# Two of a mixer chunk's 16 products delta·u·B are taken from VectorE: a transfer spreads delta·u over the states and GpSimd multiplies it by B

## The reference, cut to what matters

```python
delta = softplus(dt_r @ dt_proj_w + dt_proj_b)
dA  = exp(delta[..., None] * A)                # decay, per channel and state
dBu = delta[..., None] * Bm[:, :, None, :] * u[..., None]
h_t = dA_t * h_{t-1} + dBu_t                   # scan over the 1024 tokens
y_t = sum_n h_t[:, n] * C_t[n]   (+ u * D_param)
```

## Time and profile before

| | us |
|---|---|
| median of 3 runs (lowest, highest) | 3076.52 (3069.46, 3086.7) |
| the profiled execution, its own time | 3082.83 |
| its span in the profile | 3081.0 |
| the mixer's scans, first start to last end | 670.6 to 2519.1 |
| FFN 1 ahead of them, FFN 2 behind | 670 and 562 |
| DVE, POOL, PE busy over the span | 2644.2, 2136.8, 2641.8 |

### The profile page before, as it was taken

One profiled execution on the slowest core, in us unless ns is written; L12 is line 12 of the kernel. 1 busy time (PEld: TensorE's weight loads), 2 busy tenths in 40 slices (PEclk: granted clock), 3 DMA queues, 4 the chain that ended last, 5 costly groups with the idle time before them and its releaser, 6 DMA issues. The chain is left out here.

```text
span 3081.0 us, 31455 instructions
## 1 busy us (share of the span) xinstructions
PE 2641.8 (86%) x10275; PEld 1371.3 (45%) x10275; DVE 2644.2 (86%) x2499; ACT 1693.9 (55%) x2273; POOL 2136.8 (69%) x1284
## 2 busy tenths in 40 slices
PE   4999999967878878878878878878877669999998
PEld 2666656633324424424424424424412216666665
DVE  7888865549999999999999999999999986777775
ACT  3554444446666666666666666666664534444443
POOL 4666654258788788788788788788788755555653
PEclk9999999979969979979979979979976779999999
DMA  3011111057877777777777777776777750110100
GB/s 110 31 52 52 41 48 41 21 136 173 189 182 174 190 183 168 187 191 169 183 191 170 188 185 172 186 188 172 181 180 171 183 143 24 35 35 28 34 28 21
DMA packets 173218, 387.95 MB, mean 126 GB/s; under 512 B 22544, under 2 KB 90064, under 8 KB 172816
## 3 DMA queue, kind: packets, MB, share of 16 engines
q1 hardware_dynamic: 154176, 365.49, 47.9%
q10 hardware_dynamic: 18896, 20.65, 2.3%
HBM read 308.33 MB, written 52.56 MB: 117 GB/s over the span
## 5 line engine op out<-in xcount | busy, mean ns | idle before, releaser
L1428 POOL TENSOR_TENSOR mix_scan<-mix_scan,mix_bc 128x1024 f32<-128x1024 f32 x512 | 1205.3, 2357 | 379.0 <-DVE mix_scan L1512 378.4
L1512 DVE TENSOR_TENSOR_SCAN mix_scan<-mix_decay,ps_all 128x1024 f32<-128x1024 f32 x512 | 1170.3, 2286 | 59.9 <-ACT mix_decay L1468 16.3
L878 PE MATMUL ps_all<-ffn_w_gate_up,ffn_xT 128*128 128x512 f32 (+1 forms) x1536 | 652.6, 562 | 13.6 <-DVE ffn_h L605 9.4
L1567 PE MATMUL ps_all<-mix_stack,mix_sel 96*128 96x512 bf16 x1024 | 363.7, 443 | 349.4 <-DVE mix_scan L1512 335.4
L1468 ACT ACTIVATE mix_decay<-mix_decay,mix_a_neg 128x1024 f32<-128x1024 f32 x512 | 573.1, 1142 | 119.2 <-DMA mix_decay<-delta_rows 118.3
L1523 DVE TENSOR_TENSOR ps_all<-ps_all,mix_bc 128x1024 f32<-128x1024 f32 x512 | 617.9, 1207 | 19.4 <-PE ps_all L1567 19.3
L878 PEld LDWEIGHTS ps_all<-ffn_w_gate_up,ffn_xT 128*128 128x128 f32 x1536 | 278.5, 192 | 244.4 <-issue 199.8
L1567 PEld LDWEIGHTS ps_all<-mix_stack,mix_sel 96*128 96x128 bf16 x1024 | 76.3, 102 | 671.7 <-DVE mix_scan L1512 550.5
L605 DVE TENSOR_TENSOR ffn_h<-ffn_silu_gate,ps_all 128x704 f32<-128x704 f32 x128 | 113.7, 888 | 268.7 <-ACT ffn_silu_gate L793 265.1
L1549 PE MATMUL ps_all<-mix_scan,mix_red 128*32 128x512 f32 x2048 | 338.7, 744 | 5.4 <-POOL mix_scan L1428 5.4
L751 POOL TENSOR_TENSOR ffn_h_scaled<-ffn_h,ffn_h_recip 128x1408 f32<-128x1408 f32 x64 | 168.6, 2635 | 243.5 <-ACT ffn_h_recip L846 243.5
(11 more groups left out here) (130 smaller groups left out, 3660.3 us busy)
## 6 DMA issues: line engine op xcount, KB each, us to landing
mix_decay<-delta_rows SPq DMA_DIRECT2D x512, 512.0 KB, 7.7
mix_stack<-mix_parts SPq DMA_DIRECT2D x384, 64.0 KB, 2.0
delta_rows<-mix_delta SPq DMA_DIRECT2D x32, 512.0 KB, 3.1
ffn_x<-_attn_hidden_states_dram SPq DMA_DIRECT2D x32, 256.0 KB, 3.0
after_ffn<-ffn_y SPq DMA_DIRECT2D x32, 256.0 KB, 3.1
normed_ffn<-ffn_y_normed SPq DMA_DIRECT2D x32, 256.0 KB, 3.2
mix_x_tokens<-normed_ffn SPq DMA_DIRECT2D x32, 256.0 KB, 12.1
mix_x_residual<-after_ffn ACTq DMA_DIRECT2D x32, 256.0 KB, 5.4
```

The lines of the kernel that those rows point to most:

```text
L878: ins = M(psG[:, lo:hi], xT[:, j % 2, (t * KX + k) * P:(t * KX + k + 1) * P], wgu[:, k, lo:hi], start=(k == 0), stop=(k == KX - 1))
L1428: G.tensor_tensor(wt, wt, bc[r % 2][:, 1, :], ALU.mult).then_inc(hc_done, 1)
L1512: V.tensor_tensor_scan(w[:, slot % RING, :], da[:, slot % SPREADS, :], ps_du[:, slot % 2, :], 0.0, ALU.mult, ALU.add).then_inc(scan_done, 1)
L1567: ins = M(ps_du[:, slot % 2, h * 512:(h + 1) * 512], const.sel[0:SEL, i, :], stack[:, c % 2, q, h * 512:(h + 1) * 512], start=True, stop=True)
```

## The change

Slots 7 and 15 of each chunk (`slot % 8 == 7`) are "aside" slots: 8 in a batch, 64 in all. For them:

- PE makes no `replicate`, and DVE no product. In each chunk 14 are left.
- SP stores rows 104 to 127 of `du` to DRAM (`keep_du`, 96 KB a chunk, 32 in all) in the chunk's slot 6, ahead of the first restack, and spreads the aside slot's 8 rows over the 16 states into a new SBUF tile `aside` (`spread_du`, 512 KB, 64 in all), 6 slots ahead of its use and ahead of that slot's spread of delta. The two rows of 8 that are needed, 104 and 120, lie in what is kept.
- POOL multiplies `aside` by B, 4 slots ahead of its use: in slots 3 and 11 of a chunk, behind the product with C.
- The scan of an aside slot reads its input from `aside`, in SBUF, in place of PSUM.
- DVE runs the product of the slot behind an aside slot before the aside scan. PE makes that slot's replica one slot earlier.
- `leave1` on POOL, which overwrites `du`, waits for `keep_du` to have landed.

To make room, `sel_bc` now shares a tile with `w_dt`: the loads of the mixer's weights wait until POOL has cleared that tile, and POOL's step 5 of FFN 1, which writes the selection pattern, waits until all these loads have landed.

The diff, cut to its core:

```diff
+EVERY, ASIDE_IN, ASIDE = 8, 6, 4
+ASIDE_FROM = 104
...
+    def is_aside(slot):
+        return slot % EVERY == EVERY - 1
...
+    def du_bank(slot):
+        return (slot - (slot + 1) // EVERY) % 2
...
+    def keep_du(sy, b, par, c):
+        sy.wait_ge(du_done, chunk(b, c))
+        sy.dma_start(du_dram[par, c, :, :], du[ASIDE_FROM:P, :]).then_inc(du_kept, 16)
...
     def leave1(pool, n):
         pool.wait_ge(cast1, n)
+        pool.wait_ge(du_kept, 16 * n)
...
+            def spread_du(r, R, slot):
+                c, s = divmod(slot, SLOTS)
+                if s == EVERY - 1:
+                    sy.wait_ge(du_kept, 16 * chunk(R, c))
+                if slot >= EVERY or r > 0:
+                    sy.wait_ge(scan_done, R * 64 + (slot + 1 - EVERY))
+                row = 32 * (s % 4) + 8 * (s // 4) - ASIDE_FROM
+                sy.dma_start(aside[:, :],
+                             du_dram[r % 2, c, row:row + NCH, :].unsqueeze(0).to_broadcast([NST, NCH, L]))\
+                  .then_inc(aside_in, 16)
...
+                    rr, R2, at = ahead(r, R, slot, ASIDE_IN)
+                    if core(rr, full) and is_aside(at):
+                        spread_du(rr, R2, at)
                     rr, R2, at = ahead(r, R, slot, SPREAD)
                     if core(rr, full):
                         spread_delta(rr, R2, at)
...
+                    rr, R2, at = ahead(r, R, slot, ASIDE)
+                    if core(rr, full) and is_aside(at):
+                        pool.wait_ge(aside_in, 16 * nth_aside(R2, at))
+                        G.tensor_tensor(aside[:, :], aside[:, :], bc[rr % 2][:, 0, :], ALU.mult)\
+                         .then_inc(aside_done, 1)
...
-                dve.wait_ge(dbu_done, n)
+                if is_aside(slot):
+                    dve.wait_ge(aside_done, nth_aside(R, slot))
+                    dbu = aside[:, :]
+                else:
+                    dve.wait_ge(dbu_done, nth_vector(R, slot))
+                    dbu = ps_du[:, du_bank(slot), :]
...
-                V.tensor_tensor_scan(w[:, slot % RING, :], da[:, slot % SPREADS, :], ps_du[:, slot % 2, :], 0.0,
+                V.tensor_tensor_scan(w[:, slot % RING, :], da[:, slot % SPREADS, :], dbu, 0.0,
...
+                    if is_aside(slot):
+
+                        rr, R2, at = ahead(r, R, slot, 1)
+                        if core(rr, full):
+                            product(rr, R2, at)
+                    elif core(r, full) and slot % EVERY > 0:
+                        product(r, R, slot)
...
-                    pe.wait_ge(scan_done, R * 64 + (slot - 1))
+
+                    pe.wait_ge(scan_done, R * 64 + (slot - 1 - (1 if slot % EVERY < 2 else 0)))
...
-                    if slot == 0 and core(r, full):
-                        replicate(r, R, 0)
-                    if slot < 63 and core(r, full):
-                        replicate(r, R, slot + 1)
+                    rr, R2, at = ahead(r, R, slot, 2 if is_aside(slot + 1) else 1)
+                    if core(rr, full) and not is_aside(slot):
+                        replicate(rr, R2, at)
```

More of the change, by code:

```diff
@@ L1055, in mixer @@
     xres = a.sb("x_residual", [P, 4, 2, D])
+    aside = a.sb("dbu_aside", [P, L])
     ps_job = [bank(psum, 0), bank(psum, 7)]
@@ L1102, in job_list, with nth_aside, nth_vector @@
                 for m, (s, k, rel, n) in enumerate(mine)]
+    def is_aside(slot):
+        return slot % EVERY == EVERY - 1
+    def nth_aside(R, slot):
+        return R * (64 // EVERY) + (slot + 1) // EVERY
+    def nth_vector(R, slot):
+        return R * (64 - 64 // EVERY) + (slot + 1) - (slot + 1) // EVERY
+    def du_bank(slot):
+        return (slot - (slot + 1) // EVERY) % 2
     def nth(kind, b, n):
@@ L1301, in first_sync @@
             keep_delta(sy, 0, 0, 0)
+            keep_du(sy, 0, 0, 0)
         if k in (43, 44):
@@ L1508, in scan, with product @@
                 dve.wait_ge(exp_done, n)
-                dve.wait_ge(dbu_done, n)
+                if is_aside(slot):
[4 more added lines that the diff above has]
+                    dbu = ps_du[:, du_bank(slot), :]
                 if slot >= 8 or r > 0:
                     dve.wait_ge(y_made, R * 16 + (slot - 8) // 4 + 1)
-                V.tensor_tensor_scan(w[:, slot % RING, :], da[:, slot % SPREADS, :], ps_du[:, slot % 2, :], 0.0,
+                V.tensor_tensor_scan(w[:, slot % RING, :], da[:, slot % SPREADS, :], dbu, 0.0,
                                      ALU.mult, ALU.add).then_inc(scan_done, 1)
+            def product(r, R, slot):
+                dve.wait_ge(rep_du, nth_vector(R, slot))
+                if slot == 0:
+                    dve.wait_ge(taken["B"], (R + 1) * 4)
+                dbu = ps_du[:, du_bank(slot), :]
+                V.tensor_tensor(dbu, dbu, bc[r % 2][:, 0, :], ALU.mult).then_inc(dbu_done, 1)
             def program(r, R, full):
@@ L1564, in replicate @@
                 if slot > 1 or r > 0:
-                    pe.wait_ge(scan_done, R * 64 + (slot - 1))
+                    pe.wait_ge(scan_done, R * 64 + (slot - 1 - (1 if slot % EVERY < 2 else 0)))
                 for h in range(2):
-                    ins = M(ps_du[:, slot % 2, h * 512:(h + 1) * 512], const.sel[0:SEL, i, :],
+                    ins = M(ps_du[:, du_bank(slot), h * 512:(h + 1) * 512], const.sel[0:SEL, i, :],
                             stack[:, c % 2, q, h * 512:(h + 1) * 512], start=True, stop=True)
```

19 lines of the change are left out of this document (10 added, 9 removed).

## The result

| | before | after |
|---|---|---|
| median, us (lowest, highest; 18 runs each) | 3074.23 (3067.42, 3086.70) | 3094.68 (3090.86, 3099.89) |
| ratio after/before, 95% interval | | 1.0061 (1.0048 to 1.0074) |
| the profiled execution, its own time | 3082.83 | 3094.0 |
| first scan's start to last scan's end | 1848.4 | 1856.3 |

The change costs 20.4 us by the medians, 0.7% (0.6% by the ratio), and the interval of the ratio leaves out no change: the kernel became slower. The forecast was 3076 and no change; 3095 lies inside the range of 3040 to 3115.

The account below looks back on a forecast made before the run. The prediction took VectorE to bound the mixer, at 57.8 us a chunk. From 3082.8 us, -8 (product saved less hold) and +7 (closer waits) gave 3082; the median 6.3 lower gave 3076 us, no change, range 3040 to 3115.

Parts of the forecast that it names:

- The hold: Aside scan, both inputs in SBUF, waits for GpSimd's running instruction: 1.36 us each, ends 0 and 2.32.
- What the product gives: VectorE around an aside slot: two slots take 5.52 us instead of 7.00, saving 1.48 each, 94.7 us in all.
- "I count nothing" for the transfers: Mixer DMA: added spreads and stores make what follows land 2.2 us later, covered by ScalarE's two-slot lead; cost zero.
- the 7 us for closer waits: VectorE and GpSimd, 0.4 us a chunk apart, wait for one another: 7 us lost, between nothing and 19.
- The bound in the text: Upper limit for the added transfers: VectorE's wait for ScalarE's decay doubles, 16 us.
- The base: Starting time: profiled execution 3082.8 us, with the median of the runs 6.3 us lower.
- GpSimd's budget: GpSimd in the mixer: products, aside scans and transfer wait take 57.2 of 57.8 us a chunk.
- (a): Rival: the aside scan is not held by GpSimd; median 3011 us, chance 0.13.
- (b): Rival: aside scan held only 0.5 us, coming at the end of a GpSimd operation; median 3045 to 3060, chance 0.16.
- (c): Rival: GpSimd falls behind, scans held up to 2.32 us; median 3130 at full hold, 3100 at half, chance 0.20.
- (d): Rival: aside transfer lands at 7.7 us, not 4.6, GpSimd waits 5.3 us a chunk; median 3116, chance 0.09.

Follow-up runs that it names:

- experiment 2: Kernel before, without added transfers or GpSimd work in the mixer, but scans of slots 7 and 15 read an SBUF tile cleared once: 3152.59 us, ratio 1.0246.
- second profile: The unchanged kernel before, profiled in another execution: 3068.6 us, against 3082.83 in the profile the prediction read; scan stage 1834.4 us.
- experiment 3: Changed kernel without the delta·u stores and spreads: 3084.08 us; without GpSimd's extra products: 3078.54 us; without either: 3072.00 us.
- experiments 1: Changed kernel, but the aside scan reads the PSUM tile of the next slot's product instead of the SBUF tile: 3020.59 us, ratio 0.9822.

## Why the prediction was half right

The forecast was "no change", and the kernel became 20 us slower. The hold was foreseen; what failed is the count of the waits around it.

**The hold (mechanism right, size off by 8 us).** "I take 1.36": of VectorE's scans the aside ones are held and no others. Alone the hold measured 1.17 us (experiment 2), in the changed kernel 1.48, that is 94.6 us where 87 had been reckoned. The 64 aside scans take 3.76 us where 3.6 was written. The Trainium skill's page "SBUF — State Buffer", section "SBUF: two separate sides", says that whoever starts first gets the shared pair for the whole instruction while the other blocks. The traces agree for a scan with both inputs in SBUF (3458 ns against 2285), for a product that came 0.16 us behind a scan (4.24 us against 2.36), and show no hold with one input in PSUM (2283). Ten scans were also passed over by GpSimd instructions that had not yet started when they asked.

**What the product gives (right).** 64 × 1.48 = 94.7 us; the pitch before the aside scan is 1.14. By chance it equals the holds' 94.6: VectorE's gain is nil where 8 us had been reckoned.

**"I count nothing" for the transfers, and the 7 us for closer waits (the step that failed).** Measured against the second profile of before: wait for decays 6.7 to 25.5, that is 18.8; wait for replicas 14.7 to 18.1, that is 3.4. Together they are 22 us where 7 had been taken, and

-94.7 + 94.6 + 18.8 + 3.4 = 22.1 us, against 21.9 measured in the stage (1834.4 to 1856.3) and 20.4 in the medians of the whole program. (Outside the stage these two executions differ by another 3.5 us.) Against the first profile, which the prediction read, the same two waits grew by 9.2 and fell by 1.2, 8.0 us in all, and the stage by 7.9. So how much the waits cost depends on the execution that one starts from; the medians, with eleven of 18 runs of before in the lower group, say about 20.

The bound in the text, that VectorE's wait doubles, 16 us, was near what came. I dismissed it since the two slots that ScalarE runs ahead were to cover a spread that lands 2.2 us later. The median landing went from 7.7 to 10.4 us, about as reckoned, but the spreads behind a restack are also issued later, since the restack waits for GpSimd's `part3`. One chunk of the changed kernel, VectorE at slot 9 and SyncE:

```profile
1399.68 2.29 DVE L1572 TENSOR_TENSOR_SCAN mix_scan<-mix_decay,ps_all 128x1024 f32<-128x1024 f32 x1
```

```profile
1403.96 2.50 SPq L1162 DMA_DIRECT2D mix_stack<-mix_parts  x4
1406.50 0.59 SPq L1421 DMA_DIRECT2D mix_decay<-delta_rows  x1
1409.61 2.41 SPq L1162 DMA_DIRECT2D mix_stack<-mix_parts  x4
```

The last restack is issued 7.6 us behind the end of slot 9's scan (1409.61 - 1401.97). In the kernel before that scan is this one, and the restack of the earlier trace rows at 1400.36 comes 4.6 us behind its end:

```profile
1393.51 2.29 DVE L1512 TENSOR_TENSOR_SCAN mix_scan<-mix_decay,ps_all 128x1024 f32<-128x1024 f32 x1
```

Over the 31 `part3` that stand behind a scan, it ended 4.53 us behind its scan in the kernel before, never off by more than 0.02, and 6.88 us on average in the changed one (7.08 without transfers, 5.81 without GpSimd's product, 5.77 with neither). The same lateness shows on ScalarE, whose second cast waits for `leave1`:

```profile
L1202 ACT ACTIVATE mix_parts<-mix_delta_u x32: 1045/1057/1057, 645.8 to 2448.9; 128x1024 bf16<-128x1024 f32 x32
...
  POOL mix_delta_u L1198: 136.3, 31
```

It was 52.3 us before (49.6 in the second profile).

Where VectorE waits shows what the two slots did not cover. 15.2 of the 25.5 us stand at one place, slot 16 of a batch, 2.1 to 2.4 us in each of seven batches. ScalarE there in the second batch makes the decays of slots 15 and 16, and VectorE scans slot 16:

```profile
955.00 1.15 ACT L1523 ACTIVATE mix_decay<-mix_decay,mix_a_neg 128x1024 f32<-128x1024 f32 x1 [3.30 <-DMA mix_decay<-delta_rows]
...
960.57 1.15 ACT L1523 ACTIVATE mix_decay<-mix_decay,mix_a_neg 128x1024 f32<-128x1024 f32 x1
```

```profile
961.75 2.29 DVE L1572 TENSOR_TENSOR_SCAN mix_scan<-mix_decay,ps_all 128x1024 f32<-128x1024 f32 x1 [2.12 <-ACT mix_decay L1523]
```

ScalarE waits 3.30 us for the spread of slot 15, and between the two decays it has 4.4 us of other work (two table loads of 1.28 us, a silu and two copies), so it is late for slot 16 as well. In the kernel before it never waited for that spread. The spread was issued 7.05 us behind the end of slot 9's scan and landed 4.8 us later (second profile, means of eight batches); in the changed kernel it is issued after 11.0, since `part3` is late and the aside spread goes first, and lands 6.4 us later. So of its 5.6 us of lateness 4.0 are the queue's and 1.6 the transfer's, and the prediction had counted neither against ScalarE's work at this place. Without the transfers the two numbers are 10.4 and 4.9, without GpSimd's product 9.0 and 6.5, and ScalarE waits less; with neither they are 8.3 and 4.5 and it does not wait. The 5.3 us that VectorE still waits there with neither follow a wait of ScalarE for TensorE.

**The base (a second error).** In number it was off by little: 3082.8 less 6.3 is 3076.5, and the median is 3074.2. But the rows that the prediction weighed were those of a slower execution, with 9.6 us more waiting for decays and 4.6 more for replicas than the second profile. In six of its eight batches ScalarE waited about 3 us for TensorE (L1195) just ahead of slot 16's decay, in the second profile in two. Part of what the change would cause was already in the base, and so seemed free.

**GpSimd's budget (right).** Its wait for the aside transfer is 75.3 us (forecast 70), its wait for scans 82.5 (under 100), its share 0.92 (over 0.9). `leave1` never waited for the store. The estimate of 57.2 of 57.8 us a chunk was close enough to see that the engine would be late somewhere. That accounts for a part of the cost: GpSimd's extra products are worth 16 us and the transfers 11 (experiment 3).

**The rivals.** (a), no hold, fell in experiments 1 and 2. (b), a short hold, did not come (1.48 us and not 0.5); one aside slot in 16 comes nearer to it (0.87 us). (c), GpSimd behind, was the case on the slower side. Its time at half its price nearly came (3100, and 3094.7 measured), but of the 23 us that the stage lies above the forecast's -1 only 8 are longer holds, and 15 are waits. Its bound, "from a mean hold of 1.48 us on", is just where the chip landed, and at that hold the waits decide. (d) fell: 75 us of wait and not 170. That the range took in 3095 is owed to the half price of (c), by a mechanism that is (c)'s in part only.

**Two slips without effect.** TensorE drops 64 of 512 replicas, which are 128 of 1024 matmuls, and not 128 of 1024 replicas. And the slices just ahead of VectorE's long row of nines stand at 6, 5, 5 and 4, not at 7 or 8; they belong to FFN 1 and its end.

## What to carry to other kernels

Before work is moved from PSUM to SBUF, count which VectorE instructions end with both inputs in SBUF while GpSimd is at work, and price each at the rest of the GpSimd instruction that it will meet; one operand put into PSUM, if only the decay, removes that price. The held time is hidden in the busy time of both engines, so compare mean durations by form before looking at waits. When an engine's budget comes near the pitch, as here with 57.2 of 57.8 us, follow its other products (here the relay to the restack and the spreads queued behind it) before counting its lateness at nothing. An engine that runs two slots ahead has only as much reserve as its other work leaves in these slots. And one execution is a weak base: two of the same kernel differed here by 14 us of waiting.
